# A decoder of four layers in fp32 on one core: one query job a step in the first running group of the context attentions

## What is computed

```
q = (x @ Wq).reshape(8, 128, 32, 128);  k, v = (ctx @ Wk), (ctx @ Wv)  # 8 heads each
q, k = rope(q), rope(k)
scores = einsum('bhqd,bhkd->bhqk', q, repeat(k, 4)) / sqrt(128) + mask
attn = softmax(scores);  out = einsum('bhqk,bhkd->bhqd', attn, repeat(v, 4))
x = layernorm(x + out.reshape(8, 128, 4096) @ Wo)
```

## Time and profile before

| | us |
|---|---|
| median of 3 runs | 2548.92 |
| lowest, highest run | 2546.95, 2550.6 |
| the profiled execution, its own time | 2545.74 |
| its span | 2544.4 |
| mean granted TensorE clock of it | 0.989 |
| busy TensorE, VectorE, ScalarE, GpSimd | 2432.2, 1666.3, 992.8, 734.0 |

### The profile page before, as it was taken

One profiled execution on the slowest core, in us unless ns is written; L12 is line 12 of the kernel. 1 busy time (PEld: TensorE's weight loads), 2 busy tenths in 40 slices (PEclk: granted clock), 3 DMA queues, 4 the chain that ended last, 5 costly groups with the idle time before them and its releaser, 6 DMA issues.

```text
span 2544.4 us, 36687 instructions
## 1 busy us (share of the span) xinstructions
PE 2432.2 (96%) x12504; PEld 1523.0 (60%) x12504; DVE 1666.3 (65%) x3133; ACT 992.8 (39%) x3612; POOL 734.0 (29%) x755
## 2 busy tenths in 40 slices
PE   8999999999999798999999999998998989999998
PEld 7865666666655565456666666556664554555554
DVE  3477777777765677677777777665665644445565
ACT  0013444434444466343444444523555412323330
POOL 1037344443422111363345433222220221000002
PEclk9999999999999899999999999999999999999999
DMA  8552233222222366121333222322551020224430
GB/s 177 101 145 71 75 104 96 87 79 79 88 87 75 104 199 203 64 83 59 99 95 98 84 74 82 92 92 93 195 186 55 22 75 30 96 70 153 129 100 33
DMA packets 220378, 249.90 MB, mean 98 GB/s; under 512 B 49792, under 2 KB 165952, under 8 KB 218144
## 3 DMA queue, kind: packets, MB, share of 16 engines
q1 hardware_dynamic: 212128, 218.20, 29.1%
q10 hardware_dynamic: 8064, 29.36, 3.0%
HBM read 161.49 MB, written 85.98 MB: 97 GB/s over the span
## 4 chain that ended last, share of the span: by engine, by line
PE 84%; DVE 9%; ACT 2%; DMA 2%; issue 2%; POOL 1%; SPq 0%; DVEq 0%; ACTq 0%; POOLq 0%
PE banks L770 14%; PE banks L858 12%; PE banks L735 4%; PE banks L920 4%; PE banks L751 4%; PE banks L886 4%; PE banks L303 3%; PE banks L842 3%; PE banks L2113 3%; PE banks L1543 3%; PE banks L2164 3%; PE banks L2490 2%; PE banks L2453 2%; PE banks L2141 2%; PE banks L2183 2%
## 5 line engine op out<-in xcount | busy, mean ns | idle before, releaser
L969 ACT ACTIVATE E_x<-S_x,sm_x 128x128 f32<-128x128 f32 x512 | 199.2, 390 | 296.9 <-DVE sm_x L1143 296.9
L1205 POOL TENSOR_TENSOR QT<-QT,const 128x512 f32<-128x512 f32 x128 | 172.2, 1345 | 421.0 <-DVE turned L1023 421.0
L161 POOL TENSOR_TENSOR norm_spread<-norm_mv,const 128x1 f32<-128x1 f32 x96 | 20.9, 217 | 909.8 <-DVE norm_mv L157 909.8
L770 PE MATMUL banks<-xT,weights 128*128 128x512 f32 x512 | 235.2, 593 | 1.8 <-DVE QT L1040 1.8
L2611 ACT ACTIVATE E_s<-banks,top_s 128x128 f32<-128x128 f32 x512 | 180.5, 380 | 95.8 <-DVE top_s L2718 95.8
L1101 DVE TENSOR_TENSOR x<-banks,x 128x256 f32<-128x256 f32 (+1 forms) x288 | 147.1, 511 | 82.9 <-PE banks L858 76.8
L858 PE MATMUL banks<-weights,OT 128*128 128x256 f32 x768 | 194.9, 384 | 5.9 <-DVE weights L1084 5.9
L858 PEld LDWEIGHTS banks<-weights,OT 128*128 128x128 f32 x768 | 143.3, 190 | 68.7 <-issue 28.0
L976 ACT ACTIVATE OT<-banks 128x512 f32<-128x512 f32 x128 | 76.2, 595 | 249.3 <-PE banks L920 249.3
L1207 POOL TENSOR_TENSOR QT<-QT,turned 128x512 f32<-128x512 f32 x128 | 169.2, 1322 | 10.0
L982 ACT ACTIVATE E_x<-E_x,sm_x 128x128 f32<-128x128 f32 x512 | 162.2, 390 | 2.0 <-DVE sm_x L1157 2.0
(11 more groups left out here) (320 smaller groups left out, 4896.9 us busy)
## 6 DMA issues: line engine op xcount, KB each, us to landing
scratch_pt<-blocks_x SPq DMA_DIRECT2D x124, 256.0 KB, 2.0
PT<-scratch_pt SPq DMA_DIRECT2D x496, 64.0 KB, 2.0
scratch_latent_pt<-blocks_s ACTq DMA_DIRECT2D x56, 512.0 KB, 3.7
PT_s<-scratch_latent_pt SPq DMA_DIRECT2D x224, 128.0 KB, 3.0
weights<-in_L_xwq SPq DMA_DIRECT2D x64, 256.0 KB, 3.9
weights<-in_L_xwo SPq DMA_DIRECT2D x64, 256.0 KB, 4.3
scratch_latent_pt<-blocks SPq DMA_DIRECT2D x30, 512.0 KB, 2.6
PT<-scratch_latent_pt SPq DMA_DIRECT2D x120, 128.0 KB, 2.9
```

Of the source, the lines that this page charges most:

```text
L770: mm = PE.matmul(to, left[:, k, head], moving, start=name in ("P1", "P2", "P4", "P5") and k == 0, stop=k == 1, skip_group_check=name in (" ...
L969: ins = AC.activation(head_of(e, j, u), scores_of(s, j, u), ACT.Exp, bias=sm[:, 0, j:j + 1], scale=1.0, accum_out=sm[:, 1, j:j + 1])
L1205: PO.tensor_tensor(four(to), four(to), spread(cos128, 4), ALU.mult).then_inc(*pool_step.one())
```

## The change

Both tables get another first row, for running group 0, in which group 1 is prepared:

```
-                plans = [(1, 1, 2, 2, 1, 0, 1, 0)] + [(2, 2, 1, 2, 1, 1, 1, 0)] * (G8 - 3) + [(2, 2, 1, 2, 1, 0, 0, 0)]
+                plans = [(1, 1, 1, 1, 1, 1, 1, 1)] + [(2, 2, 1, 2, 1, 1, 1, 0)] * (G8 - 3) + [(2, 2, 1, 2, 1, 0, 0, 0)]
...
-                shares = [(1, 1, 2, 1, 1, 1, 1, 0)] + [(0, 1, 1, 2, 1, 1, 1, 1)] * (G8 - 2)
+                shares = [(1, 1, 1, 1, 1, 1, 1, 1)] + [(0, 1, 1, 2, 1, 1, 1, 1)] * (G8 - 2)
```

## The result

| us | before | changed |
|---|---|---|
| median | 2549.39 (2545.2 to 2551.52, 6 runs) | 2559.27 (2554.66 to 2564.44, 6 runs) |
| ratio, 95% interval | | 1.0054 [1.0040, 1.0067] |
| the profiled execution, its span | 2545.74, 2544.4 | 2554.66, 2553.3 |

The account below looks back on a forecast made before the run. TensorE, busy 96% of the span, was taken as the bound, time being lost in its waits or lower clock. The terms 4.5 + 1.6 + 3.2 + 1.6 = +10.9 on the median 2548.92 gave 2559.8, range 2551 to 2566.

Parts of the forecast that it names:

- Fetches become visible: Steps 2 and 3: TensorE waits 2.0 us ahead of mix(1) for the transposed blocks fetched back from DRAM.
- q4 behind the exponentials: Step 4: q4's third product waits 3.2 us for ScalarE's bank copy, which now stands behind the exponentials.
- The SyncE queue: Step 5: fetch(3) stands behind the weight load, which waits for q5; TensorE waits 6.2 us at mix(3), the largest term.
- the first rival: Same waits, cheaper: fetch(3) lands in 2.2, not 4.4, and the clock stays up; +3.3, 2552.2; chance 0.13.
- The sums of OT: Steps 5 to 7: TensorE waits 0.6 us for VectorE's sums of OT, in place of 2.50.
- The clock: Lower TensorE clock after the 6.2 wait costs 2.2 us, +1.6 a stage net; none after the 3.2 of step 4.
- the third rival: The clock falls twice, also at the 3.2 wait of step 4: 3.8 a stage, +15.3, 2564.2; chance 0.15.
- The second rival: Faster: old waits go and TensorE finds everything ready, if fetch(3) is back before mix(3); -5.6 and -5.0, 2538.3; chance 0.07.
- The old waits: Steps 2 to 7 before: TensorE's four waits for QT additions, ScalarE's copy and sums of OT; 5.6 in stage 1.
- the ceiling of 10.6: Largest possible gain, in us, if one job a step removed all TensorE waits in both stretches and made nothing new.

Follow-up runs that it names:

- the rotations alone: Kernel before with only the sine parts moved, one pair in each step, jobs as before: 2542.43 against 2544.65, ratio 0.9990.
- the last experiment: Changed kernel with q3 beside q2 in step 2, q4 in step 3, q5 in step 4: 2537.70 against 2545.86 of the kernel before, ratio 0.9960.

## Why the prediction was right

The forecast was +10.9 on the median of 2548.92. The medians here differ by 9.9, by the ratio it is 13.8, and the two stretches of the traces grew by 12.7. By its steps:

- **Fetches become visible**, 2.0: 1.61 and 1.63 in the trace.
- **q4 behind the exponentials**, 3.2: 2.91 and 2.72. The sine pair of VectorE ahead of it took 0.89 + 1.67 = 2.6, where 2.8 was assumed (rows below the list).
- **The SyncE queue**, 6.2: 5.57 and 5.48. From the first weight DMA to mix(3) are 268.44 - 261.18 = 7.3, not 7.8, since the fetch landed 4.0 after its issue, not 4.4; the first rival needed 2.2. That this queue is the cause is shown both ways: its order put right removes the loss (1.0003), its wait put into the kernel before makes it (1.0054).
- **The sums of OT**, 0.6, which was to disappear under the fall of the clock: none. That VectorE had time for them while TensorE waited and ran slowly is argued, not shown.
- **The clock**, 2.2 at mix(3) and none in q4: this term failed, and here the third rival had the mechanism. The granted clock fell at both waits in both stages (windows of the changed kernel: length, then busy PE, PEld, DVE, ACT, POOL, PEclk, DMA):

```profile
248.60:251.80 3.20, 3.16 (x4) 1.31 (x5) 0.27 (x1) 0.00 (x0) 0.00 (x0) 0.58 0.00 1
268.40:272.00 3.60, 3.56 (x6) 2.16 (x7) 0.00 (x0) 1.45 (x5) 3.37 (x4) 0.50 0.22 60
1133.40:1136.80 3.40, 3.36 (x5) 1.52 (x6) 0.28 (x1) 0.00 (x0) 0.00 (x0) 0.54 0.00 1
1152.90:1157.00 4.10, 4.01 (x9) 2.62 (x9) 0.19 (x1) 1.76 (x5) 3.87 (x4) 0.50 0.22 64
```

Mix(3) to v0 took 273.37 - 268.44 = 4.9 in stage 1, where 0.86 + 0.86 + 0.89 = 2.6 is the work at full clock: 2.3 lost. q4's last product and the products behind it lost 1.8. That is 4.1 in stage 1, and 3.7 in stage 4 by the same rows. The prediction had 2.2 for the one fall and nothing for the other; rival three had 1.7 + 2.7 = 4.4, which is nearer. (The fall after the 2.03 before, put at 1.7, cost 1.5 by the same work in stage 1.)

The sine pair, on VectorE's timeline and beside it on GpSimd's:

```profile
242.41 0.89 DVE L1022 TENSOR_TENSOR turned<-QT,const 64x512 f32<-64x512 f32 x1
243.31 1.67 DVE L1023 TENSOR_TENSOR turned<-QT,const 64x512 f32<-64x512 f32 x1
```

```profile
241.49 1.27 POOL L1205 TENSOR_TENSOR QT<-QT,const 128x512 f32<-128x512 f32 x1
242.84 1.60 POOL L1207 TENSOR_TENSOR QT<-QT,turned 128x512 f32<-128x512 f32 x1
```

At their shortest in this trace L1207 takes 1.27 and L1023 0.69. Counted back from the ends with these times, L1207 began its own work at 243.17, 0.13 before L1022 ended, and L1023 at 244.29, 0.15 before L1207 ended. So the two engines took turns, each starting a little before the recorded end of the other, and a sine instruction took 1.67 and not 0.68 + 1.27 = 1.95. The turns agree with the lock, held for a whole instruction, of the Trainium skill (SBUF — State Buffer, "SBUF: two separate sides"). The prediction was right to keep the 1.67 of its row.

So the forecast met the time by two errors of opposite sign. The prediction's sum counts a wait from the end of the work ahead, at full-clock prices, to the next start, some 0.16 more than the idle time of a row. Counted so, the three waits are 10.6 in stage 1 and 10.3 in stage 4, against 2.0 + 3.2 + 6.2 = 11.4, too long by 0.8 and 1.1. The clock was priced too low by 1.9 and 1.5. Together that is 1.1 and 0.4 more a stage, about what the stretches show (7.3 and 5.4 against 6.1 and 4.8). That they nearly cancel is luck. The step on the clock was the weakest of the prediction, and the total doesn't show it.

The second rival, faster, failed by the condition that it named: 1.73 us of work stood between q5 and mix(3). The old waits did all go, as it said. Once the new ones are kept from forming there is a gain, 8.9 in the stretches of the last experiment. It is made up differently from the ceiling of 10.6: 0.87 and 1.69 of waits a stage are left there, and 1.5 is the fall of the clock in stage 4 before, which the ceiling left out.

## What to carry to other kernels

A table that moves the jobs of one engine also moves the waits of a queue whose own order stays the same. For each transfer that waits for a job, ask which transfers stand behind it in the same queue and how far ahead of their use they still are. Here the two issues in the other order took the loss away (1.0003); with ScalarE's copy moved as well, or with one job a step earlier and no other edit, the change turned from 0.5% slower to 0.4% faster.

## What was not expected

Whether the clock falls after a wait can't be told from its length alone. With the fetch ahead of the load, the wait inside q4 was 2.80 in stage 1 and 2.68 in stage 4, with the same work around it. After the first, four records took 1.98 at a granted clock of 1.00, after the second 3.56 at 0.54 (windows, the same columns):

```profile
247.40:251.00 3.60, 3.56 (x13) 2.40 (x14) 1.05 (x3) 0.60 (x1) 0.00 (x0) 1.00 0.26 73
1126.90:1130.50 3.60, 3.58 (x5) 1.54 (x6) 0.25 (x1) 0.00 (x0) 0.00 (x0) 0.54 0.25 73
```

In the changed kernel nearly the same waits, 2.91 and 2.72, were both followed by the lower level. The fall need not come at once either. With the rotations alone, stage 1, products at full clock stood between the wait of 1.94 and the fall:

```profile
271.70 1.13 PE L858 MATMUL banks<-weights,OT 128*128 128x256 f32 x4 [1.94 <-DVE weights L1084]
```

```profile
271.60:272.60 1.00, 0.90 (x4) 0.82 (x5) 0.13 (x2) 0.00 (x0) 0.00 (x0) 1.00 0.23 67
272.60:276.90 4.30, 4.30 (x12) 2.81 (x11) 2.06 (x3) 1.76 (x5) 1.76 (x2) 0.60 0.16 46
```

Over the two stretches of all nine traces, the 18 waits from 1.36 to 1.87 were followed by no fall and the 10 of 4.91 and more each by one. Of the seven between, 1.94, 2.03, 2.68, 2.72 and 2.91 were followed by one, 2.50 and 2.80 were not. A fall after one of these cost 1.5 to 1.8, as much as many of the waits themselves. What decides between 1.9 and 3 stays open. So a stretch of a single trace can be 1.5 to 1.8 longer or shorter by such a fall; the ratios rest on several executions.

Not tried: the fetch at mix(1) put on another queue, and the 1.69 that VectorE's sums of OT still cost in the fastest version.
